# Where the scan's decay factors lie and who makes the second chunk's step sizes, in a Mamba, GPTQ and MoE kernel on one core

## The reference, cut to what matters

```python
proj = hidden_states @ W_in.T                # x and gate, 1024 channels each
x = silu(conv4(x) + conv_b)
ts, Bm, Cm = rms(x @ W_x.T)                  # 32, 16 and 16 wide
dt = softplus(ts @ W_dt.T + b_dt)            # step sizes
def step(state, inp):                        # state: [b, 1024, 16]
    dA = exp(dt_t[..., None] * A)
    state = state * dA + (dt_t * u_t)[..., None] * B_t[:, None, :]
    return state, einsum('bdn,bn->bd', state, C_t)
y = (ys + x * D) * silu(gate)
return y @ W_out.T
# second layer: gate = x @ Wg; up = x @ Wu; (gate * sigmoid(gate) * up) @ Wd
```

## Time and profile before

| what | value |
|---|---|
| median of 3 runs | 831.85 us |
| profiled execution | 831.04 us, span 828.8 us |
| busy: TensorE, VectorE | 688.4 us (83%), 691.8 us (83%) |
| busy: ScalarE, GpSimd | 463.1 us (56%), 491.7 us (59%) |
| scans: first to last start | 57.7 to 487.2 us |

### The profile page before, as it was taken

The page is one execution under the profiler, slowest core; times in us unless marked ns, Lnnn a source line. Parts: engine busy times, 40 slices in busy tenths (PEclk is TensorE's granted clock), DMA queues, the critical chain, the costliest instruction groups (busy, mean ns, idle before and its releaser), DMA issues. The chain is left out here.

```text
span 828.8 us, 8406 instructions
## 1 busy us (share of the span) xinstructions
PE 688.4 (83%) x2790; PEld 327.1 (39%) x2790; DVE 691.8 (83%) x696; ACT 463.1 (56%) x778; POOL 491.7 (59%) x257
## 2 busy tenths in 40 slices
PE   8969759998767788556646869999999999999993
PEld 7623213333212222111112223444444546787882
DVE  6789889989999999998999998998274565595668
ACT  4565786797655775866654543766325346323421
POOL 2419999989999999999999940110002014340151
PEclk9998979999958998857757979999999999999998
DMA  8333122330543514630235219962030030000011
GB/s 271 74 109 122 66 103 91 128 127 25 203 131 126 192 63 165 203 127 28 100 127 177 77 29 246 258 172 75 1 152 1 1 102 1 1 1 1 1 51 51
DMA packets 42001, 82.39 MB, mean 99 GB/s; under 512 B 6743, under 2 KB 10240, under 8 KB 41704
## 3 DMA queue, kind: packets, MB, share of 16 engines
q1 hardware_dynamic: 41960, 81.87, 31.0%
HBM read 70.65 MB, written 11.21 MB: 99 GB/s over the span
## 5 line engine op out<-in xcount | busy, mean ns | idle before, releaser
L2205 POOL TENSOR_TENSOR dbu<-rep_du,bc 128x1024 f32<-128x1024 f32 x127 | 297.4, 2366 | 22.6 <-ACT rep_du L1882 19.4
L1748 ACT ACTIVATE psum<-rep_dt,aneg 128x512 f32<-128x512 f32 x256 | 166.2, 682 | 123.7 <-DVE hc L1151 101.0
L1140 DVE TENSOR_TENSOR_SCAN psum<-psum,dbu 128x1024 f32<-128x1024 f32 x87 | 198.8, 2285 | 8.0 <-ACT psum L1748 6.4
L914 PE MATMUL psum<-hc,stk 128*32 128x512 f32 x512 | 84.5, 737 | 58.4 <-POOL hc L2214 34.3
L1151 DVE TENSOR_TENSOR hc<-psum,bc 128x1024 f32<-128x1024 f32 x87 | 106.5, 1224 | 3.4 <-PE psum L914 0.4
L2214 POOL TENSOR_TENSOR hc<-hc,bc 128x1024 f32<-128x1024 f32 x41 | 96.5, 2353 | 8.8 <-DVE hc L1140 8.3
L1140 DVE TENSOR_TENSOR_SCAN hc<-psum,dbu 128x1024 f32<-128x1024 f32 x41 | 93.5, 2281 | 7.4 <-PE psum L914 2.8
L673 PE MATMUL psum<-xf_hi,gu_hi 128*128 128x512 f16 x176 | 66.8, 379 | 1.0 <-ACT sg L2040 1.0
L673 PE MATMUL psum<-xf_lo,gu_hi 128*128 128x512 f16 x176 | 66.7, 379 | 0.0
L673 PE MATMUL psum<-xf_hi,gu_lo 128*128 128x512 f16 x176 | 66.7, 379 | 0.0
L673 PE MATMUL psum<-xT,w_g 128*128 128x512 f32 x120 | 60.1, 648 | 6.9 <-ACT rep_du L1882 5.0
(11 more groups left out here) (267 smaller groups left out, 1453.6 us busy)
## 6 DMA issues: line engine op xcount, KB each, us to landing
rep_dt<-rep_scratch SPq DMA_DIRECT2D x60, 256.0 KB, 3.4
rep_du<-rep_scratch SPq DMA_DIRECT2D x60, 256.0 KB, 4.3
cw<-c_scratch SPq DMA_DIRECT2D x11, 768.0 KB, 7.6
qw<-qgu_in SPq DMA_DIRECT2D x11, 512.0 KB, 4.7
bc<-bc_scratch SPq DMA_DIRECT2D x16, 256.0 KB, 4.6
rep_scratch<-du_t SPq DMA_DIRECT2D x15, 256.0 KB, 2.0
rep_scratch<-dt_t SPq DMA_DIRECT2D x15, 256.0 KB, 2.3
qw<-qd_in SPq DMA_DIRECT2D x11, 256.0 KB, 5.4
```

What stands on the lines that cost most here:

```text
L914: last = pe.matmul(y_rows(k), stk[:], hc[:, (i + k // 2) % HCS, k % 2, :], start=False, stop=(s == GN - 1))
L1140: dve.tensor_tensor_scan(h, a, dbu[:, i % DBS].rearrange("p e t -> p (e t)"), 0.0, ALU.mult, ALU.add)\
L1748: last = act.activation(psum[:, 2 * (i % 2) + e, :], rep_dt[:, cc % 2, k, :], ACT.Exp, scale=aneg[:, k, c, n:n + 1])
L2205: pool.tensor_tensor(dbu[:, i % DBS], rep_du[:, cc % 2, k:k + 2, :], bc[:, n, :].unsqueeze(1).broadcast_to([P, 2, L]), ALU.mult).then_inc( ...
```

## The change

It does six things.

1. At six places the Silu moves by 0 to 2 pairs (`SILU_AT` = 8, 16, 32, 41, 64, 73), and the Exps of the pair after it (`SPARE` = 9, 17, 33, 42, 65, 74) are issued just before it, into a tile in SBUF (`spare_a`). The other pairs take turns in the PSUM banks without these. All six are pairs whose product with C is on GpSimd.
2. Chunk 1's step sizes are a product of the ring, `("dt", 1)`. ScalarE makes all four steps of its softplus before the first pair; GpSimd adds, multiplies and resets (three instructions) before its first `times_b`. `second_steps` is gone.
3. `gate(0, 0)` moves from ahead of the step sizes to the other two gates, behind the spreads.
4. `keep_clock` makes 7, 2, 2, 2 and 6 products of the identity in place of 12, 3, 3, 3 and 8.
5. Chunk 10 has two pairs on GpSimd in place of three; the four additions of `obuf` to x (L2242) are issued at four pairs, one each, in place of two at two pairs.
6. At the start of the feed-forward block VectorE has `unpack(2)` before `low_weights(1)`, `scaled(2)` before the first `ffn_times`, and `ffn_low(0, 0)` right behind it.

```diff
-POOL_MORE = (0, 1, DC + 2)
+POOL_MORE = (0, 1)
+POOL_LESS = (DC + 2,)
+SILU_AT = (QP, 2 * QP, 4 * QP, 5 * QP + 1, 8 * QP, 9 * QP + 1)
+SPARE = tuple(i + 1 for i in SILU_AT)
...
+def in_psum(i):
+    return [j for j in range(i + 1) if j not in SPARE]
+def a_slot(i):
+    return len(in_psum(i - 1)) % 2
...
-            keep_clock(12)
+            keep_clock(7)
...
-                keep_clock(3 if t < NT - 1 else 8)
+                keep_clock(2 if t < NT - 1 else 6)
...
-            gate_half(0, 0, 0)
-            gate_half(0, 0, 1)
...
             dt_part(0)
-            dt_second()
+            dt_part(1)
...
-            for c in range(1, GATES_FIRST):
+            for c in range(GATES_FIRST):
                 gate_part(0, c)
...
-                two = slice(2 * (i % 2), 2 * (i % 2) + 2)
-                a = psum[:, two, :].rearrange("p e t -> p (e t)")
+                two = slice(2 * a_slot(i), 2 * a_slot(i) + 2)
+                a = (spare_a[i] if i in SPARE else psum[:, two, :]).rearrange("p e t -> p (e t)")
...
-                if i == 2:
-                    second_steps()
...
+            unpack(2)
             low_weights(1)
-            unpack(2)
+            scaled(2)
...
                 if i == 0:
-                    scaled(2)
+                    ffn_low(0, i)
...
-            keep_gate(0, 0)
             sp_abs(0)
...
-                if i >= 2:
+                if i >= 2 and i not in SPARE:
                     decay(i)
...
+                if i in SILU_AT:
+                    decay(i + 1)
...
+            pool.tensor_tensor(dt1_log[:], dt1_log[:], dt1_pos[:], ALU.add).then_inc(dt1_sum, 1)
+            pool.wait_ge(dt1_sum, 1)
+            pool.tensor_tensor(du1[:], dt1_log[:], u0[:, 1, :], ALU.mult).then_inc(dut_ready, 1)
```

More of the change, by code:

```diff
@@ L121, in pe_order @@
     items = [("tr", "ssm", 0, t) for t in range(NT)] + [("x", 0, c) for c in range(DC)]
-    items += [("ms", 0), ("gate", 0, 0), ("dt", 0)] + [("spread", k) for k in range(1, KH)]
-    items += [("gate", 0, c) for c in range(1, GATES_FIRST)]
+    items += [("ms", 0), ("dt", 0), ("dt", 1)] + [("spread", k) for k in range(1, KH)]
+    items += [("gate", 0, c) for c in range(GATES_FIRST)]
     for cc in range(NCH):
@@ L259, in build @@
         dt1_pos = at("dt1_pos", 195, [L])
+        du1 = at("du1", 197, [L])
+        spare_a = dict(zip(SPARE, (at(f"spare_a{n}", k, [2, L]) for n, k in enumerate([151, 151, 151, 195, 195, 187]))))
         obuf = [at("obuf0", 195, [NT, H]), at("obuf1", 141, [NT, H])]
@@ L391, in build @@
         first_dbu = sem("first_dbu")
-        dt1_ready = sem("dt1_ready")
-        dt1_taken = sem("dt1_taken")
         dt1_sum = sem("dt1_sum")
@@ L819, in spread_du @@
                 spread_one(du_t, k, bank(item)).then_inc(work_ready, 1)
-            def dt_second():
-                pe.matmul(psum[:, KH - 1, :], wdt[0:2 * R + 1, P:2 * P], ssmn[0:2 * R + 1, :], start=True, stop=True)\
-                    .then_inc(dt1_ready, 1)
-            def gate_half(b, c, h):
-                item = ("gate", b, c)
-                if h == 0:
-                    start(item)
-                for k in range(2 * h, 2 * h + 2):
-                    last = pe.matmul(bank(item), w_g[:, k, c * P:(c + 1) * P], xT[:, k, :], start=(k == 0),
-                                     stop=(k == KH - 1))
-                if h == 1:
-                    last.then_inc(work_ready, 1)
             for c in range(DC):
@@ L1727, in free_pair @@
             def free_pair(i):
-                if i >= 2:
-                    if on_pool(i - 2):
-                        act.wait_ge(scan_done, i - 1)
+                if i in SPARE:
+                    return
+                if len(in_psum(i - 1)) >= 2:
+                    j = in_psum(i - 1)[-2]
+                    if on_pool(j):
+                        act.wait_ge(scan_done, j + 1)
                     else:
-                        act.wait_ge(cmul_done, dve_c(i - 2))
+                        act.wait_ge(cmul_done, dve_c(j))
             def decay(i):
@@ L1747, in decay @@
                     k = 2 * (q % 2) + e
-                    last = act.activation(psum[:, 2 * (i % 2) + e, :], rep_dt[:, cc % 2, k, :], ACT.Exp,
-                                          scale=aneg[:, k, c, n:n + 1])
+                    out = spare_a[i][:, e, :] if i in SPARE else psum[:, 2 * a_slot(i) + e, :]
+                    last = act.activation(out, rep_dt[:, cc % 2, k, :], ACT.Exp, scale=aneg[:, k, c, n:n + 1])
                 last.then_inc(exp_done, 1)
@@ L1967, in _ @@
                     inv_rms(1)
-                if i == 7:
+                if i == SILU_AT[0]:
                     silu_gates(0, 0)
-                if i == 2 * QP:
+                if i == SILU_AT[1]:
                     silu_gates(0, 1)
-                if i == pair_of(("cv", 1, 3)) + 5:
+                if i == SILU_AT[2]:
                     silu_u(0)
-                if i == pair_of(("cv", 1, 7)) + 5:
+                if i == SILU_AT[3]:
                     silu_u(1)
-                if i == pair_of(("gate", 1, 3)) + 9:
+                if i == SILU_AT[4]:
                     silu_gates(1, 0)
-                if i == pair_of(("gate", 1, 7)) + 7:
+                if i == SILU_AT[5]:
                     silu_gates(1, 1)
-                if i in (7, 2 * QP, pair_of(("cv", 1, 3)) + 5, pair_of(("cv", 1, 7)) + 5,
-                         pair_of(("gate", 1, 3)) + 9, pair_of(("gate", 1, 7)) + 7):
+                if i in SILU_AT:
                     act.preload_act_table_set(LOG_EXP)
@@ L2237, in _ @@
                     dt_times_u((i - 6) // QP + 2)
-                if i in (pair_of(("out", 0, NT - 1)) + 9, pair_of(("out", 0, NT - 1)) + 11):
-                    first = i - pair_of(("out", 0, NT - 1)) - 9
-                    for t in range(first, first + 2):
-                        pool.wait_ge(on_ready, t + 1)
-                        pool.tensor_tensor(x[:, t, :], x[:, t, :], obuf[0][:, t, :], ALU.add).then_inc(out_done, 1)
+                t = i - pair_of(("out", 0, NT - 1)) - 9
+                if 0 <= t < NT:
+                    pool.wait_ge(on_ready, t + 1)
+                    pool.tensor_tensor(x[:, t, :], x[:, t, :], obuf[0][:, t, :], ALU.add).then_inc(out_done, 1)
             for t in range(NT):
```

45 lines of the change are left out of this document (20 added, 25 removed).

## The result

The changed kernel takes 836.78 us in the median of 5 runs (836.12 to 837.33), the kernel before 832.36 (831.83 to 834.46) beside it: a ratio of 1.0046, 95% interval 1.0028 to 1.0063. It is slower. The forecast was 831.6, no change, with 823.5 to 836.5 around it; the median lies 0.3 us above that.

What follows compares the result with a forecast made beforehand. VectorE and GpSimd were taken to bound the scan together, with TensorE joining in chunks 2 to 4. The terms summed to -0.2 us, 830.8 for 831.04 profiled, or 831.6 against the median; range 828 to 835, wide 823.5 to 836.5.

Steps and rivals of the forecast that it cites:

- The late spare scans: Scans 42, 65 and 74: waits for GpSimd cost +2.9 us; the last Silu's wait goes, -1.0.
- the size at scan 9: Spare scan 9 waits for the GpSimd product at hand, +1.7 us.
- the price of 42: Spare scan 42 falls 0.1 us behind a GpSimd product's start; priced at half of 2.33 us.
- the slower rival: Spare scans come just behind a GpSimd product's start; GpSimd also gives 2.1 us at each; 837.3 us, chance 0.21.
- Chunk 10 and the additions: Late scan: one product moves from GpSimd to VectorE and VectorE's waits before 376.82 go, -1.2 us.
- The start: Up to scan 9: fewer identity products -1.8, gate(0, 0) moved -0.9, lower clock +0.5, gate's new place +0.9 us.
- The term for the low clock: At the step size product: TensorE, now idle before it, runs it at 1.2 GHz, +0.5 us.
- the 76.9 of the prediction: Scan 4: VectorE waits until 76.9 us for TensorE's first sum behind twelve gate products.
- Scans 17 and 33, TensorE's run: Chunks 2 to 4: Silu gains and both scans' waits vanish in VectorE's slack against TensorE, 0.
- within 1 us: Sign that the forecast is right: TensorE's dense run to chunk 4 begins within 1 us of 122.6.
- The feed-forward start: Start of the feed-forward block: TensorE's 2.00 us wait for it_lo goes, 0.7 comes back, -1.3 us.
- The rival "just behind GpSimd's start": Scans 9, 42, 65 and 74 each wait 2.33 us, 9.3 in place of 4.6; 837.3 us, chance 0.21.

Runs made afterwards that it cites:

- e13: Changed kernel with GpSimd's next product held until a due spare scan has ended; 1.0072 of the kernel before.
- e9: Changed kernel with six more spare pairs (45, 49, 52, 54, 58, 61), their decay factors in SBUF; 1.0177 of the kernel before.
- e12: Changed kernel with spare pairs 9, 17 and 33 only, the last three Silus in their old places; 1.0006 of the kernel before.
- e3: Changed kernel with no spare tiles, all decay factors in PSUM and the six Silus in their old places; 1.0025 of the kernel before.
- e6: Kernel before with only chunk 10, the additions and the start of the feed-forward block changed; 0.9986 of the kernel before.
- e7: Changed kernel with 18 more identity products where TensorE waits in the start; 1.0047 of the kernel before.
- e10: Changed kernel, gate(0, 0) ahead of step sizes, eight identity products behind; spare tiles only 9, 17, 33, GpSimd held there; last three Silus in old places; 0.9955 of before.
- e15: e10 without the hold on GpSimd; 0.9947 of the kernel before.
- e14: The changed kernel itself, unaltered, timed and profiled a second time; 1.0062 of the kernel before.
- e5: Kernel before with only the edit at the start of the feed-forward block; 0.9988 of the kernel before.
- e16: e10 with 23 more identity products on TensorE at the end of the scan; 0.9938 of the kernel before.
- e17: Kernel before with 23 more identity products on TensorE at the end of the scan; 0.9992 of the kernel before.

## Why the prediction was wrong, step by step

*The late spare scans (+2.9, less 1.0 for the Silu).* This is the step that decided. That a spare scan and an instruction of GpSimd exclude each other was right (e13, e9), and so was the size at scan 9 (+1.7; the scan took 1.72 longer, the position grew by 1.88) and at 65 (0.5, measured 0.47). By the Trainium skill, SBUF — State Buffer, Who interferes with whom, a VectorE instruction with two SBUF inputs contends with a GpSimd instruction that reads SBUF, for a port pair that is locked for a whole instruction; the traces agree, with 4.38 us for a scan and 4.3 us for a product of GpSimd that take 2.3 alone.

Wrong was the price of 42, put at half a product though its own row stood 0.1 us behind the start of one: it stood so again and paid 2.10. And the forecast priced only VectorE's side. GpSimd's 2 us behind pair 74 had no term in its sum, only in the slower rival. They are not hidden. GpSimd works without a break from 299 us to its product with C of pair 77 (the expectations call it pair 78), so it brings them there. TensorE's sum of pairs 76 and 77 needs that product and starts 2.0 us later against the scans: at +7.8 and +6.9 in the two traces, where scan 80 stands at +5.8 and +4.9; in e12 it is +1.3 for both. TensorE then makes the output product at the lower clock, and VectorE waits for the next sum, 1.11 us in the first trace and 2.39 in the second. GpSimd's three products, the sum and the output product before (the last row is for the feed-forward part):

```profile
307.83 6.97 POOL L2205 TENSOR_TENSOR dbu<-rep_du,bc 128x1024 f32<-128x1024 f32 x3
...
327.07 1.06 PE L914 MATMUL psum<-hc,stk 128*32 128x512 f32 x8 [1.16 <-POOL hc L2214]
328.07 7.13 PE L673 MATMUL psum<-wout,g 128*128 128x512 f32 x16
...
493.58 7.68 PE L673 MATMUL psum<-wout,u 128*128 128x512 f32 x14 [0.81 <-DVE u L1167]
```

Sum and output product in the changed kernel's second trace (the first has 4.83 and 8.22):

```profile
333.92 1.94 PE L910 MATMUL psum<-hc,stk 128*32 128x512 f32 x8 [6.11 <-POOL hc L2203]
335.79 9.20 PE L685 MATMUL psum<-wout,g 128*128 128x512 f32 x16
```

From scan 38 to 104 the position grows by 3.87 and 5.07 in the two traces of the changed kernel; with the three pairs undone (e12) it falls by 0.99. So they cost 4.9 to 6.1 us net, where the forecast had 1.9, and the ratio comes to 1.0006 without them. That the waits at 70 and at 82 hang on the late pairs is shown by their absence in e3 and e12; as both put the last Silus back too, the share of the Silus' places is not separated. At scan 42 it is: in e13 the Silu and the tile stay, only GpSimd is held, and the 2.1 us are gone. How much each of the three pairs adds was not tried.

*Chunk 10 and the additions (-1.2).* The saving is real, 0.95 in e6, 0.96 in e3, 0.97 in e12. In the changed kernel the wait of pair 82 stands in front of it. Mis-sized by the step above, not by itself.

*The start (-1.8, -0.9, +0.5, and +0.9 at scan 9).* The sum has -2.2 by ScalarE's first copy of `rep_dt`; measured is +0.40 (55.96 against 55.56). The input products were 0.76 us sooner at the end, not 1.8, and part of this is chance: they begin at 13.4 to 14.3 us in the four traces with the start of before. Leaving the gate out gave 0.8, as forecast: the step sizes begin 1.58 sooner (48.84 against 50.42). The term for the low clock, +0.5, was the mis-sized one: the first step size product cost 1.0 more, and the spreads, which had no term, another 1.0, with the granted clock at 0.50 from 49 to 65 us.

Scan 4 came at 76.54, near the 76.9 of the prediction, but by luck. The 76.9 is reckoned on the start of before; with the -2.2 the forecast was 74.7. The gates began 0.49 later than before in place of 2.2 sooner, and took 12.09 us in place of 13.0, since the clock rose sooner behind their start. The second trace and e7 show how little of an earlier start passes this place: scan 0 came 1.07 and 3.04 us sooner than in the first trace, the gates took 13.29 and 13.50, and scan 4 came 0.13 later and 0.74 sooner. At scan 9 the miss is 1.8 (+0.47 for -1.3).

*Scans 17 and 33, TensorE's run (0).* The waits of the two scans stayed without effect on scan 38 in the first trace (-0.13); in the second the stretch gave 1.1 us. The run began 1.8 us later than before (124.45), not within 1 us. That it swallows what came before is not general: e10 and e15 carried 2 to 2.5 us of an earlier start through it.

*The feed-forward start (-1.3).* The wait of 2.00 went in the first trace, as forecast, and 0.7 was to come back; 0.76 came, at 530.49 (1.21 in e14, 0.69 in e5). The other 1.3 can't be seen at the end either: the output products took 9.35 us in place of 7.68, at the lower clock for longer, and in e14, where they took 8.16, the waits were longer instead. e16 shows the same of a faster TensorE there: it then waits for VectorE's weights. By the times of e5 a gain of up to 1.8 us is possible; this term stays open.

Of the 6.3 us between the forecast sum and the traces, 1.8 come from the start, 1.7 from the late pairs up to scan 80, 1.5 from pair 82, behind which chunk 10's saving is lost, and 1.3 from the feed-forward block.

The rival "just behind GpSimd's start" (837.3, outside the stated range) came nearest to the time. Its condition, a mean wait above 1.8, was met in neither trace (1.72, 2.10, 0.47 and 0.27 in the first, a mean of 1.1; 1.5 in the second, with 1.70 at 74), and the difference came as waits of VectorE for TensorE. That its number fits is luck.

## What to carry to other kernels

Before an operand moves from PSUM to SBUF, look at whether the instruction then has both inputs there and what GpSimd does at that moment; price both engines, and follow the one that is made late to whoever waits for it. A part is worth what is left at the next place where another engine binds: 3.04 us at scan 0 became 0.74 at the first sum (e7), and 1.4 us of TensorE 0.5 (e17). When a forecast position comes true, see whether its terms did. And profile a kernel twice before a difference of 1 us between two traces is put down to an edit.
